# Second-norm rows ahead of the gated output, and the gate kept in PSUM, in a two-layer transformer kernel

## The chip, the cores and the metric

One core of a Trainium2 chip runs the whole program. The metric is the device time of one execution in microseconds. A core has TensorE (PE, with its weight loads PEld), VectorE (DVE), ScalarE (ACT), GpSimd (POOL) and SyncE (SP, which here issues DMAs), two on-chip memories (SBUF and PSUM, the second with 8 banks) and DMA queues. The engines run on their own and wait for each other by semaphores.

## What is computed

Two layers, each an attention and a mixture of experts, each behind an adaptive layer norm, on x of 8 x 512 rows by 256 columns (4096 rows, 32 tiles of 128). The change touches the first attention and the norm behind it:

```python
h = _layernorm(x, axis=-1) * (1 + ca) + sa
x = x + ga * _L0_attn_ref(h, W_Q, W_K, W_V, W_O)      # gated output, summed into x
h = _layernorm(x, axis=-1) * (1 + cb) + sb            # second norm: the "rows"

def _L0_attn_ref(query, W_Q, W_K, W_V, W_O):
    ...
    cos_KV = jnp.cumsum(cos_k * V, axis=1)
    sin_KV = jnp.cumsum(sin_k * V, axis=1)
    heads = cos_q * cos_KV + sin_q * sin_KV
    ...
    heads = heads / denom
    return jnp.einsum('deh,bthe->btd', W_O, heads)
```

`ga`, `sb` and `cb` are one row per batch entry, that is, per four tiles.

## The kernel before

Fp32 products are made of fp16 pairs: each operand is split into a high part and the low remainder (ScalarE rounds the high part, GpSimd subtracts it to get the low one), and three products are summed. X stays in SBUF for the whole program.

The first attention goes over 32 tiles in one loop, `for i in range(NT)`, written out by hand once for each engine. Nothing plans the order: it is the order of the lines in each engine's function, and semaphores tie them. In iteration i:

- TensorE (`tensor`) sums the scaled values of tile i along the sequence with a triangular matrix, in banks 0 to 3 (`tri`, 8 matmuls of 512 columns); turns the heads of tile i-1 (`turn_heads`, 8 transposes); multiplies the values of tile i+2 (`values`, 12 matmuls); except at a batch's end (i % 4 == 3), adds the rest of the tile into the banks for the next tile (`atri`, 8 matmuls), once VectorE has read the sums; projects the heads of tile i-1 (`heads_out`, 24 matmuls of 256 columns); at a batch's end it also spreads the second norm's scale and shift over the partitions (`by_batch`).
- VectorE (`vector`) reads the four banks and multiplies them by the queries' cosine and sine into TM (four instructions), makes the low part of tile i-1's turned heads (`heads_lo`, two), scales the first half of tile i+2's values (`spread`, two; these eight have 512 columns each), and adds the two halves of TM (1024 columns, both in SBUF; the head addition). Then `attended(i - 1)`: the gate (the projection in PSUM times GB, into the SBUF ring YG0), the add into X, and the moments of the new row (`moments`, two instructions); every fourth tile `factor`, a reciprocal of four columns. Last `rows(i - 5)` (R_AFTER is 5): two instructions that make the normed and modulated rows of a tile in the ring HR0.
- ScalarE (`scalar`) rounds the rows of tile i-6 (`rows_hi`) and the turned heads (`heads_hi`), scales the second half of the values of tile i+2 in 16 instructions, rounds the four pieces of the scaled values (`spread_hi`), takes a square root for a batch's four rows when their moments are there (`root`), and, from i = 3 to 26, rounds one piece of the experts' weights (`convert`, 1024 columns).
- GpSimd (`gpsimd`) makes the low parts of the same: `rows_lo` (256 columns), `spread_lo` (four of 512 columns) and `convert` (1024). Each reads two tensors in SBUF.
- SyncE loads and stores the pieces of the experts' weights, paced by GpSimd's `convert`, and stores the rows' pairs; after the loop, once the last projection is done, it loads the experts' weights.

The values, the projection and the spread scale and shift share two PSUM banks, 4 and 5, in a fixed order `VR`; `vr_free` (line 781) says what TensorE waits for before it writes a bank again. For a bank that held a projection that is the gate: `yg` counts two per tile, the gate and the add.

In the profile, VectorE's tensor-tensor instructions have line L1301 (the helper `tt`), told apart by shape and tiles: `BIG<-ps,BIG 128x256` is the gate, `X<-X,BIG` the add, `BIG<-BIG 128x1024` the head addition. L1447 and L1450 are the two instructions of `rows`, L1308 and L1310 the moments, L1315 the reciprocal. GpSimd's have L2297, ScalarE's scaling L1926 and its other copies L1852. TensorE's products have L736, its transposes in this loop L853. BIG is the large SBUF array of which most buffers are views, and ps is PSUM.

Of the kernel before, what the change touches and what calls it, by code (L numbers as in the profile page):

```python
# [8 lines left out]
ALU = mybir.AluOpType  # L9
# [3 lines left out]
B, S, D = 8, 512, 256  # L13
# [41 lines left out]
def bc(ap, axis, n):  # L55
    a = ap.unsqueeze(axis)
    shape = list(a.shape)
    shape[axis] = n
    return a.broadcast_to(shape)
# [9 lines left out]
def program(nc, x_in, wqk_in, wv_in, wo_in, rw_in, rb_in, w1_in, w3_in, w2_in, c0_in, m0_in,  # L69
# [3 lines left out]
    with ctx:  # L73
        def sb(name, shape, dt=fp32):
            return ctx.enter_context(nc.sbuf_tensor(name, shape, dt))
# [4 lines left out]
        s = {n: ctx.enter_context(nc.semaphore(n)) for n in SIGNALS}  # L80
# [12 lines left out]
        X = sb("X", [128, NT, D])  # L93
# [23 lines left out]
        ps = [ctx.enter_context(nc.psum_tensor(f"ps{i}", [128, 512], fp32)) for i in range(8)]  # L117

        def view(off, *shape, dt=None, parts=128):
            n = math.prod(shape)  # L120
            words = n // 2 if dt == f16 else n
            assert off + words <= BIGW, (off, shape)
            v = BIG[0:parts, off:off + words]
            return shaped(v.bitcast(dt) if dt is not None else v, shape)
# [35 lines left out]
        area = Area(22912)  # L160
# [4 lines left out]
        area = Area(0)  # L165
# [4 lines left out]
        cv_st, cv_pr = area.ring(2, 1024), area.pairs(2, 1024)  # L170

        cks = view(cv_at + 2048, 2, 2, NT, 16, dt=f16)
        YG0 = area.ring(2, D)
        GB = area(8, D)
        lap = area.at
        assert lap <= 22912, lap
        area = Area(lap)
# [18 lines left out]
        def kv_made(i, hf, j):  # L196

            if not by_act(i):
                return "kvf", 4 * i + 2 * hf + j + 1
            return ("kva", "kvf")[hf == 0], (8 if hf == 0 else 0) + 2 * (i - 2) + j + 1  # L200


        R_AFTER, R_SPLIT = 5, 6
# [24 lines left out]
        def heads_of(ap):  # L228
            return ap.rearrange("p (h e) -> p h e", e=64)
# [8 lines left out]
        vr_no = {u: i for i, u in enumerate(VR)}  # L238
# [117 lines left out]
        for l in range(2):  # L356
# [3 lines left out]
                y=[0, 0] if l == 0 else [16 * len(range(k, M[0].NS, 2)) for k in range(2)],  # L360
# [7 lines left out]
        area = Area(0)  # L368
# [18 lines left out]
        area = Area(33792)  # L387
        OI, OIT = area.ring(2, D), area.ring(2, 2, 2, 128, dt=f16)
        assert area.at <= 35584
        area = Area(35584)  # L390
        HF.append(area.pair(2, 2048))

        area = Area(36992)
# [338 lines left out]
        def tensor(e):  # L732
            pe = Lane(e)
# [47 lines left out]
            def vr_free(u):  # L781
                n = vr_no[u]
                if n < 2:
                    pe.wait_ge(s["modc"], 3)
                    return
                kind, i, hf = VR[n - 2]
                if kind == "v":
                    made, k = kv_made(i, hf, 1)
                    pe.wait_ge(s[made], k)
                elif kind == "s":  # L790
                    pe.wait_ge(s["sc"], i + 1)
                else:
                    pe.wait_ge(s["yg"], 2 * i + 1)

            def values(i):
                for hf in range(2):
# [11 lines left out]
            for t in range(A_TICKS):  # L808
                if t == T_PART:
                    mod_columns(1)  # L810
                if t in T_GB:
                    p = T_GB.index(t)
# [54 lines left out]
            for i in range(NT):  # L867
# [30 lines left out]
                if i % 4 == 3:  # L898
                    u = ("s", i // 4, 0)
                    vr_free(u)  # L900
                    pe.wait_ge(s["modg"], 8)
                    by_batch(ps[4 + vr_no[u] % 2], 0, 2, 4, i // 4).then_inc(s["sc_ps"], 1)
# [394 lines left out]
        def vector(e):  # L1297
            dve = Lane(e)

            def tt(o, a, b, op):  # L1300
                return e.tensor_tensor(o, a, b, op)  # L1301

            def moments(n, i):

                r = n % 4
                if n >= 4:
                    dve.wait_ge(s["bn"], 2 * (n - 4) + 2)
                e.bn_stats(bnst[:, r, :], X[:, i, :]).then_inc(s["bn"], 1)  # L1308
                dve.wait_ge(s["bn"], 2 * n + 1)
                e.bn_aggr(stat[:, i, :], bnst[:, r, :]).then_inc(s["bn"], 1)  # L1310

            def factor(g, dev):

                dve.wait_ge(s["rs_a"], g + 1)
                e.reciprocal(dev, dev).then_inc(s["rs_v"], 1)  # L1315
# [6 lines left out]
            def row(i):  # L1322
                return rstd[:, i - 3:i + 1]
# [31 lines left out]
            def divide(h):  # L1355

                cut = slice(16 * h, 16 * h + 16)
                cumc, cums = (cumb[h][:, j].rearrange("p b c n -> p (b c) n") for j in range(2))
                dn, d2 = (TH[:, cut, :].rearrange(FLAT)[:, 256 * k:256 * k + 256].rearrange("p (t n) -> p t n", n=16) for k in range(2))
                dve.wait_ge(s["kc_ps"], h + 1)  # L1360

                dve.wait_ge(s["th"], 3 * h + 3)
                c = Serial(dve, s["dn"], 6 * h)
                tt(dn, QC[:, cut, 0:16], cumc, ALU.mult).then_inc(c.next(), 1)
                n = c.next()
                tt(d2, QS[:, cut, 0:16], cums, ALU.mult).then_inc(n, 1)
                n = c.next()
                e.scalar_tensor_tensor(out=dn, in0=dn, scalar=1e-6, in1=d2, op0=ALU.add, op1=ALU.add).then_inc(n, 1)
                n = c.next()
                e.reciprocal(dn, dn).then_inc(n, 1)  # L1370
                n = c.next()
                tt(QC[:, cut, 0:16], QC[:, cut, 0:16], dn, ALU.mult).then_inc(n, 1)
                n = c.next()
                tt(QS[:, cut, 0:16], QS[:, cut, 0:16], dn, ALU.mult).then_inc(n, 1)
# [42 lines left out]
            def heads_lo(i):  # L1417
                for q in range(2):
                    dve.wait_ge(s["ht_hi"], 2 * i + q + 1)
                    tt(HT[i % 2][1][:, 4 * q:4 * q + 4, :], ps[6 + q][:, :].rearrange("p (j n) -> p j n", j=4),  # L1420
                       HT[i % 2][0][:, 4 * q:4 * q + 4, :], ALU.subtract).then_inc(s["ht_lo"], 1)

            def attended(i):
                dve.wait_ge(s["pr_ps"], i + 1)
                dve.wait_ge(s["gr"], 4)
                if i >= 2:
                    dve.wait_ge(s["yg"], 2 * (i - 2) + 2)
                tt(YG0[i % 2], ps[4 + vr_no["p", i, 0] % 2][:, 0:256], GB[:, i // 4, :], ALU.mult).then_inc(s["yg"], 1)
                dve.wait_ge(s["yg"], 2 * i + 1)
                tt(X[:, i, :], X[:, i, :], YG0[i % 2], ALU.add).then_inc(s["yg"], 1)  # L1430
                dve.wait_ge(s["yg"], 2 * i + 2)
                moments(NT + i, i)
                if i and i % 4 == 0:
                    factor(8 + i // 4 - 1, row(i - 1))

            def rows(n):

                b = n // 4
                dve.wait_ge(s["rs_v"], 8 + b + 1)
                dve.wait_ge(s["sc"], b + 1)  # L1440
                if n >= 4:
                    dve.wait_ge(s["hs_lo"], n - 3)
                else:

                    dve.wait_ge(s["dn"], 12)
                h, sc = HR0[n % 4], SC[b % 2]
                e.scalar_tensor_tensor(out=h, in0=X[:, n, :], scalar=stat[:, n, 0:1], in1=sc[:, 256:512],  # L1447
                                       op0=ALU.subtract, op1=ALU.mult).then_inc(s["hr"], 1)
                dve.wait_ge(s["hr"], 2 * n + 1)
                e.scalar_tensor_tensor(out=h, in0=h, scalar=rstd[:, n:n + 1], in1=sc[:, 0:256],  # L1450
                                       op0=ALU.mult, op1=ALU.add).then_inc(s["hr"], 1)

            for i in range(NT):
                dve.wait_ge(s["cum"], i + 1)
                dve.wait_ge(s["dn"], 6 if i < 16 else 12)
                if i >= 2:
                    dve.wait_ge(s["hdT_ps"], 2 * (i - 2) + 2)
                tm = TM[i % 2]
                for j, q in ((0, QC), (1, QS)):
                    for hf in range(2):  # L1460
                        tt(heads_of(tm[:, j, hf * 512:hf * 512 + 512]), heads_of(ps[2 * j + hf][:, :]),
                           bc(q[:, i, 8 * hf:8 * hf + 8], 2, 64), ALU.mult).then_inc(s["rd"], 1)
                if i:
                    heads_lo(i - 1)
                if i + 2 < NT:
                    spread(i + 2)
                dve.wait_ge(s["rd"], 4 * i + 4)
                tt(tm[:, 0], tm[:, 0], tm[:, 1], ALU.add).then_inc(s["hd"], 1)
                if i == 0:
                    divide(1)  # L1470
                if i:
                    attended(i - 1)
                if i >= R_AFTER:
                    rows(i - R_AFTER)
            heads_lo(NT - 1)


# [1112 lines left out]

        block = ctx.enter_context(nc.Block())
        block.vector(vector)
        block.sync(sync)
        block.gpsimd(gpsimd)
# [32 lines left out]
```

## Time and profile before

| what | value |
|---|---|
| median of 3 runs | 1909.5 us (1907.44 to 1913.1) |
| the profiled execution, its own time | 1908.69 us |
| its span | 1906.9 us |
| TensorE busy in the span | 1605.1 us (84%) |
| VectorE busy | 1180.3 us (62%) |
| GpSimd busy | 1088.0 us (57%) |
| ScalarE busy | 968.2 us (51%) |
| DMA | 204.16 MB, mean 107 GB/s |

The span runs from the first to the last instruction of the profiled execution; the rest of its time lies around it. Busy times overlap, so their shares say only how full an engine is over the whole program, whose stages differ. The attention loop that the change touches runs from about 76 to 462 us of the span; routing, the first experts (from 548 us), the second attention, and the second experts follow.

### The profile page before, as it was taken

To read this page: it belongs to the slowest core of one execution; us is meant where nothing else is said; L and a number is where in the kernel's file an instruction comes from. 1 tells how busy PE (TensorE), PEld (TensorE's weight loads), DVE (VectorE), ACT (ScalarE), POOL (GpSimd) and SP (SyncE) were. 2 spreads that over 40 slices of the span, in tenths; PEclk is the share of its full clock that TensorE was granted. 3 is DMA by queue.
4 is the path that set the end of the run, shared out by engine and by line. 5 is a ranking of instruction groups with operands and counts; after the bars stand their busy time and mean duration, and the time that the engine had idled before them with its cause. 6 is when DMAs were issued, how large, how long until landed. Compare 5 with 4: busy or idle time off the path is not lost.

```text
span 1906.9 us, 38349 instructions
## 1 busy us (share of the span) xinstructions
PE 1605.1 (84%) x13740; PEld 1179.2 (62%) x13740; DVE 1180.3 (62%) x1766; ACT 968.2 (51%) x2400; POOL 1088.0 (57%) x949
## 2 busy tenths in 40 slices
PE   6798878877799999999999927878887867599992
PEld 5454444445688888888888813334443325599992
DVE  7777787777543333333444376899999998422224
ACT  6675665564344444444454347544443436355553
POOL 5566556653133333333453289899997995355543
PEclk9899898899599999999999966989998997699996
DMA  5013332311733333333343150011110244366665
GB/s 200 23 45 97 100 93 83 100 59 61 263 95 101 101 99 100 98 99 98 115 157 95 51 176 23 1 28 29 29 29 25 73 146 125 132 237 245 232 236 185
DMA packets 130625, 204.16 MB, mean 107 GB/s; under 512 B 44864, under 2 KB 90960, under 8 KB 125328
## 3 DMA queue, kind: packets, MB, share of 16 engines
q1 hardware_dynamic: 114368, 132.22, 22.1%
q0 software_dynamic: 16080, 69.48, 10.8%
q8 instruction: 123, 2.02, 0.4%
q14 instruction: 54, 0.44, 0.1%
HBM read 138.09 MB, written 63.57 MB: 106 GB/s over the span
## 4 chain that ended last, share of the span: by engine, by line
PE 57%; DVE 17%; POOL 12%; issue 7%; ACT 2%; DMA 2%; SPq 0%; POOLq 0%; DVEq 0%; ACTq 0%
PE ps L736 55%; POOL BIG L2297 10%; DVE BIG L1301 9%; DVE X L1301 2%; DVE BIG L1801 2%; DMA BIG<-YT 1%; ACT BIG L1852 1%; DVE bnst L1308 1%; DVE BIG L1447 1%; POOL BIG L2501 1%; PE ps L1017 1%; POOL X L2297 1%; DVE BIG L1779 1%; PE ps L1086 0%; DMA BIG<-HB,BIG 0%
## 5 line engine op out<-in xcount | busy, mean ns | idle before, releaser
L736 PE MATMUL ps<-BIG 128*128 128x256 f16 (+9 forms) x11272 | 1294.7, 289 | 142.0 <-DVE BIG L1301 52.1
L736 PEld LDWEIGHTS ps<-BIG 128*128 128x128 f16 (+3 forms) x11272 | 973.1, 101 | 427.8 <-issue 77.1
L2297 POOL TENSOR_TENSOR BIG<-BIG 128x256 f16<-128x256 f32 (+6 forms) x547 | 751.6, 1406 | 488.1 <-ACT BIG L1852 466.9
L1852 ACT ACTIVATE BIG<-BIG 128x512 f16<-128x512 f32 (+3 forms) x543 | 329.9, 658 | 300.4 <-DVE BIG L1301 181.5
L1301 DVE TENSOR_TENSOR BIG<-BIG 128x512 f16<-128x512 f32 (+9 forms) x334 | 265.9, 804 | 273.7 <-ACT BIG L1852 266.3
L1852 ACT ACTIVATE BIG<-ps 128x64 f32<-128x64 f32 (+7 forms) x791 | 275.5, 409 | 266.1 <-PE ps L736 236.2
L1301 DVE TENSOR_TENSOR BIG<-ps,BIG 128x512 f32<-128x512 f32 (+3 forms) x421 | 290.4, 745 | 82.0 <-PE ps L736 80.6
L1301 DVE TENSOR_TENSOR BIG<-BIG,ps 128x512 f32<-128x512 f32 (+2 forms) x212 | 125.0, 594 | 262.7 <-PE ps L736 246.6
L2439 POOL DMA_INDIRECT YT<-BIG x109 | 108.7, 998 | 191.1 <-ACT BIG L1852 190.4
L1801 DVE TENSOR_REDUCE BIG<-BIG 128x160 f32<-128x2560 f32 x64 | 182.0, 2843 | 0.0
L2433 POOL DMA_INDIRECT BIG<-HB,BIG x109 | 108.3, 994 | 70.0 <-DVE BIG L1301 38.6
L2210 ACT ACTIVATE ps<-ps 128x512 f32<-128x512 f32 x64 | 37.2, 582 | 138.9 <-PE ps L736 138.9
L1926 ACT ACTIVATE BIG<-ps,BIG 128x64 f32<-128x64 f32 x480 | 101.4, 368 | 12.4 <-PE ps L736 12.0
L2068 ACT ACTIVATE BIG<-ps 128x512 f32<-128x512 f32 x140 | 81.9, 585 | 12.1 <-PE ps L736 12.1
L736 PE MATMUL ps<-BIG,atri 128*128 128x512 f16 x192 | 52.8, 425 | 29.3 <-DVE BIG L1301 29.3
L2117 ACT ACTIVATE BIG<-ps 128x512 f32<-128x512 f32 x78 | 46.6, 597 | 41.8 <-PE ps L736 38.7
L1779 DVE TENSOR_REDUCE BIG<-ps 128x32 f32<-128x512 f32 x64 | 43.7, 682 | 33.3 <-PE ps L736 32.4
L736 PE MATMUL ps<-BIG,tri 128*128 128x512 f16 (+1 forms) x264 | 63.1, 377 | 0.9 <-DVE BIG L1301 0.9
L2217 ACT ACTIVATE BIG<-ps 128x512 f32<-128x512 f32 x64 | 38.4, 600 | 36.6 <-DVE BIG L1801 36.5
L736 PEld LDWEIGHTS ps<-BIG,atri 128*128 128x128 f16 x192 | 18.9, 107 | 61.3 <-DVE BIG L1301 38.4
L1308 DVE BATCH_NORM_STATS2 bnst<-X 128x6 f32<-128x256 f32 x128 | 54.2, 423 | 3.9 <-DMA X<-in_x 2.1
L2468 POOL DMA_INDIRECT BIG<-WG,BIG x39 | 37.3, 955 | 27.0 <-DVE BIG L1301 13.5
(139 smaller groups left out, 955.6 us busy)
## 6 DMA issues: line engine op xcount, KB each, us to landing
WD<-BIG SPq DMA_DIRECT2D x80, 256.0 KB, 2.4
BIG<-in_v SPq DMA_DIRECT2D x32, 512.0 KB, 4.6
BIG<-in_w SPq DMA_DIRECT2D x24, 512.0 KB, 4.0
BIG<-WD SPq DMA_DIRECT2D x32, 384.0 KB, 7.6
BIG<-YT SPq DMA_DIRECT2D x24, 512.0 KB, 5.0
HB<-BIG SPq DMA_DIRECT2D x64, 128.0 KB, 2.5
WG<-BIG SPq DMA_DIRECT2D x32, 256.0 KB, 3.2
BIG<-WD SPq DMA_DIRECT2D x16, 512.0 KB, 5.3
```

The lines of the kernel that those rows point to most:

```text
L736: return e.matmul(o, lhsT, rhs, start=start, stop=stop, skip_group_check=True)
L1301: return e.tensor_tensor(o, a, b, op)
L1308: e.bn_stats(bnst[:, r, :], X[:, i, :]).then_inc(s["bn"], 1)
L1779: e.tensor_reduce(SM[q % 4], shaped(ps[2 + q % 3][:, :], (2, 16, 16)), AX.X, ALU.max).then_inc(s["sm"], 1)
L1801: e.tensor_reduce(OB[c % 2][:, 2 * q2:2 * q2 + 2], PV[q % 2], AX.X, ALU.add).then_inc(s["vr"], 1)
L1852: return e.activation(o, i, ACT.Copy)
L1926: o = e.activation(KVF[i % 2][:, j, 512 + 64 * h:576 + 64 * h], ps[4 + vr_no["v", i, 1] % 2][:, 64 * h:64 * h + 64], ACT.Copy, scale=q[:, ...
L2068: e.activation(m_.UP[u % 2], ps[2 * u % 4][:, :], ACT.Silu).then_inc(s["su"], 1)
L2117: e.activation(m_.UP[j % 2][:, hf * 512:hf * 512 + 512], ps[idx % 4][:, :], ACT.Gelu).then_inc(s["su"], 1)
L2297: return e.tensor_tensor(o, a, b, op)
L2433: e.indirect_dma_start(m_.HIN[t % ring], None, m_.HB, bass.IndirectOffsetOnAxis(m_.gi[:, t:t + 1], 0)).then_inc(ld_hi[t % ring], 16)
L2439: e.indirect_dma_start(m_.YT, bass.IndirectOffsetOnAxis(m_.yi[:, t:t + 1], 0), m_.YO[t % 2], None).then_inc(st_y[t % 2], 16)
```

## The change

In VectorE's loop the order behind the head addition becomes: the reciprocal of the batch before (in iterations 5, 9, 13 and so on, as before, but ahead of the rest), the rows of tile i-5, and then the gate, the add and the moments of tile i-1. The gate writes its result over the projection in PSUM instead of into the SBUF ring YG0, and the add into X reads it there. YG0 (512 words per partition) goes, and so does the wait for it; the buffers placed behind it move down. TensorE waits for the add instead of the gate before it writes that bank again.

```diff
@@ -170,7 +170,6 @@
         cks = view(cv_at + 2048, 2, 2, NT, 16, dt=f16)
-        YG0 = area.ring(2, D)
         GB = area(8, D)
@@ -790,7 +789,7 @@
                 else:
-                    pe.wait_ge(s["yg"], 2 * i + 1)
+                    pe.wait_ge(s["yg"], 2 * i + 2)
@@ -1423,15 +1422,12 @@
             def attended(i):
                 dve.wait_ge(s["pr_ps"], i + 1)
                 dve.wait_ge(s["gr"], 4)
-                if i >= 2:
-                    dve.wait_ge(s["yg"], 2 * (i - 2) + 2)
-                tt(YG0[i % 2], ps[4 + vr_no["p", i, 0] % 2][:, 0:256], GB[:, i // 4, :], ALU.mult).then_inc(s["yg"], 1)
+                y = ps[4 + vr_no["p", i, 0] % 2][:, 0:256]
+                tt(y, y, GB[:, i // 4, :], ALU.mult).then_inc(s["yg"], 1)
                 dve.wait_ge(s["yg"], 2 * i + 1)
-                tt(X[:, i, :], X[:, i, :], YG0[i % 2], ALU.add).then_inc(s["yg"], 1)
+                tt(X[:, i, :], X[:, i, :], y, ALU.add).then_inc(s["yg"], 1)
                 dve.wait_ge(s["yg"], 2 * i + 2)
                 moments(NT + i, i)
-                if i and i % 4 == 0:
-                    factor(8 + i // 4 - 1, row(i - 1))
@@ -1468,10 +1464,12 @@
                 if i == 0:
                     divide(1)
+                if i % 4 == 1 and i > 1:
+                    factor(8 + i // 4 - 1, row(i - 2))
+                if i >= R_AFTER:
+                    rows(i - R_AFTER)
                 if i:
                     attended(i - 1)
-                if i >= R_AFTER:
-                    rows(i - R_AFTER)
             heads_lo(NT - 1)
```

## Rows read from the trace of the kernel before

**Rows 1.** The page: the span.
```profile
span 1906.9 us, 38349 instructions
```

**Rows 2.** Busy time by stretch; columns: stretch, its length, each engine's busy us, clock, DMA.
```profile
98.50:127.50 29.00, 27.49 (x182) 17.48 (x181) 22.95 (x40) 21.61 (x69) 16.15 (x14) 1.00 0.12 38
...
179.60:231.20 51.60, 41.73 (x240) 24.65 (x240) 40.83 (x62) 31.80 (x100) 31.61 (x25) 0.90 0.31 92
...
548.00:1066.00 518.00, 518.00 (x4865) 461.73 (x4863) 207.17 (x264) 237.78 (x392) 201.12 (x168) 1.00 0.34 106
```

**Rows 3.** VectorE's groups, 89 to 480 us: busy us, mean ns of one, idle before.
```profile
L1450 DVE SCALAR_TENSOR_TENSOR BIG<-BIG,rstd 128x256 f32<-128x256 f32 x32 | 37.2, 1161 | 1.1
L1301 DVE TENSOR_TENSOR X<-X,BIG 128x256 f32<-128x256 f32 x32 | 33.9, 1059 | 1.1
...
L1301 DVE TENSOR_TENSOR BIG<-ps,BIG 128x256 f32<-128x256 f32 x32 | 13.6, 425 | 74.7 <-PE ps L736 74.7
```

**Rows 4.** VectorE in order of time, iterations 11 to 15: start us, duration us, instruction.
```profile
203.47 4.86 DVE L1301 TENSOR_TENSOR BIG<-ps,BIG 128x512 f32<-128x512 f32 x8
...
216.78 0.45 DVE L1447 SCALAR_TENSOR_TENSOR BIG<-X,stat,BIG 128x256 f32<-128x256 f32 x1
217.27 0.48 DVE L1450 SCALAR_TENSOR_TENSOR BIG<-BIG,rstd 128x256 f32<-128x256 f32 x1
217.67 4.87 DVE L1301 TENSOR_TENSOR BIG<-ps,BIG 128x512 f32<-128x512 f32 x8
222.46 1.22 DVE L1301 TENSOR_TENSOR BIG<-BIG 128x1024 f32<-128x1024 f32 x1
225.43 0.42 DVE L1301 TENSOR_TENSOR BIG<-ps,BIG 128x256 f32<-128x256 f32 x1 [1.75 <-PE ps L736]
...
228.93 4.87 DVE L1301 TENSOR_TENSOR BIG<-ps,BIG 128x512 f32<-128x512 f32 x8
...
239.81 2.23 DVE L1450 SCALAR_TENSOR_TENSOR BIG<-BIG,rstd 128x256 f32<-128x256 f32 x1
...
254.98 1.28 DVE L1301 TENSOR_TENSOR BIG<-ps,BIG 128x512 f32<-128x512 f32 x2
```

**Rows 5.** GpSimd in order of time, in iterations 12 and 13.
```profile
223.14 5.08 POOL L2297 TENSOR_TENSOR BIG<-BIG 128x512 f16<-128x512 f32 x4 [4.18 <-ACT BIG L1852]
...
238.15 3.60 POOL L2297 TENSOR_TENSOR BIG<-BIG 128x512 f16<-128x512 f32 x2
```

**Rows 6.** All engines in order of time, iterations 3 and 4, which make no rows.
```profile
108.07 4.88 DVE L1301 TENSOR_TENSOR BIG<-ps,BIG 128x512 f32<-128x512 f32 x8
...
113.00 2.79 PE L736 MATMUL ps<-BIG 128*128 128x256 f16 x24 [1.51 <-DVE BIG L1301]
...
118.00 4.88 DVE L1301 TENSOR_TENSOR BIG<-ps,BIG 128x512 f32<-128x512 f32 x8 [0.38 <-PE ps L736]
...
120.16 2.13 POOL L2297 TENSOR_TENSOR BIG<-BIG 128x1024 f16<-128x1024 f32 x1
...
121.47 3.38 ACT L1926 ACTIVATE BIG<-ps,BIG 128x64 f32<-128x64 f32 x16 [1.94 <-PE ps L736]
...
125.44 2.46 POOL L2297 TENSOR_TENSOR BIG<-BIG 128x512 f16<-128x512 f32 x2 [3.16 <-ACT BIG L1852]
125.61 1.89 PE L736 MATMUL ps<-BIG,tri 128*128 128x512 f16 x8
125.81 0.42 DVE L1301 TENSOR_TENSOR BIG<-ps,BIG 128x256 f32<-128x256 f32 x1 [1.80 <-PE ps L736]
...
127.54 0.69 DVE L1301 TENSOR_TENSOR BIG<-ps,BIG 128x512 f32<-128x512 f32 x1
```

**Rows 7.** The page's groups: ScalarE from PSUM to PSUM, and to SBUF.
```profile
L2210 ACT ACTIVATE ps<-ps 128x512 f32<-128x512 f32 x64 | 37.2, 582 | 138.9 <-PE ps L736 138.9
...
L2217 ACT ACTIVATE BIG<-ps 128x512 f32<-128x512 f32 x64 | 38.4, 600 | 36.6 <-DVE BIG L1801 36.5
```

**Rows 8.** VectorE in order of time: the start of iteration 30.
```profile
443.39 3.67 DVE L1301 TENSOR_TENSOR BIG<-ps,BIG 128x512 f32<-128x512 f32 x6
```

## The prediction

> **What bounds the kernel now.** I read five things in turn: the span, the busy table of the attention loop, the groups of VectorE's instructions there, one stretch of the loop in order of time, and the five iterations that have no second-norm rows yet. The profiled execution took 1908.69 us, 1.79 us of it outside its span [rows 1]; the median of the three runs shown is 1909.5, so I sum against 1908.7 and add 0.8.
>
> In a stretch of 51.6 us of the loop no engine is full: TensorE is busy 41.7 us, VectorE 40.8, ScalarE 31.8, GpSimd 31.6, and TensorE's granted clock is 0.90 [rows 2]. So a chain across engines sets the pace. Four iterations (i = 11 to 14) run from 203.47 to 254.98: 51.5 us, 12.9 each [rows 4].
>
> The chain stands in one iteration in order of time [rows 4]. It starts at S, when VectorE begins to read the cumulative sums. Eight instructions follow, then the addition of the two heads' halves, finished at S+6.0 (217.67 to 223.68). VectorE then idles 1.75 us until TensorE's projection of the tile before is there (225.43, S+7.8), gates it, adds it into X, takes moments, makes the rows, and only then starts the next iteration (228.93). The rows stand behind the late arrival although their inputs are five tiles old.
>
> Two kinds of instruction on that chain last much longer than their work. The add into X takes 1059 ns in the mean, the gate of the same shape, which reads one operand from PSUM, 425; the rows' second instruction takes 1161 in the mean [rows 3] and 0.48 at its shortest [rows 4]. Where it took 2.23 (239.81 to 242.04), GpSimd was running two subtractions from 238.15 to 241.75 [rows 5]: VectorE ended 0.3 us behind it. An instruction whose two tensors both lie in SBUF waits for GpSimd's current one; the gate never does, since 425 is the mean of all 32.
>
> Iterations 3 and 4, which make no second-norm rows, show what the loop can do without this [rows 6]. Iteration 4 lasted 9.54 us (118.00 to 127.54) and iteration 3 9.93 (108.07 to 118.00); the second has no `atri` product and ends a batch, and TensorE waited 1.51 us in it. TensorE's cumulative sum for iteration 5 ran 125.61 to 127.50, straight behind its projection, and VectorE started at 127.54: both engines are full there, at clock 1.00 [rows 2]. That is the floor: 9.54 for three iterations of four, 9.93 for the fourth.
>
> **The change, part by part.** Rows are made in iterations 5 to 31.
>
> (a) The rows move into the idle time. Uncontended they cost 0.45 + 0.48 = 0.93 us [rows 4], once in four with a reciprocal of four columns more (some 0.1 us, an estimate), against 1.75 us idle: S+6.0 to S+7.0 or 7.1. Behind the projection there remain gate, add, moments. In iteration 4 this chain lasted 125.81 to 127.54, 1.73 us, with an add of 0.60.
>
> (b) The add reads PSUM and X: one SBUF tensor, so the shape of the gate, 0.425 [rows 3]. That takes 0.63 off its mean, and 0.18 off the chain just named: 1.73 - 0.18 = 1.55. VectorE could start again at S+7.8+1.55 = S+9.35, before TensorE's sum at 9.5. So TensorE sets the pace.
>
> (c) The gate writes PSUM. No VectorE row of this loop does. The nearest pair is ScalarE's, PSUM to PSUM 582 ns against PSUM to SBUF 600 [rows 7]. I take 0.42; bounds 0.40 and, doubled, 0.85. The double would make the chain 1.98 and the iteration 9.8. Adding the same doubt for the add's PSUM read gives 10.2.
> The Trainium skill (VectorE: DVE Perf Modes, the section on the TRN2 errata) gives a PSUM source 62 cycles more than an SBUF one, some 0.065 us, which speaks against moving the operand. The trace doesn't show it for this shape: the gate takes 0.425 [rows 3], and the add in iterations 1 to 4 was no shorter. By the page the chain is 1.62 instead of 1.55, 27 times 0.065 or 1.8 us if all of it were exposed, and nothing of it under the 9.54 floor.
>
> (d) Does GpSimd leave that gap free? It depends on when its hi/lo subtractions start. Now they start at 223.14, S+5.5 [rows 5], because VectorE is late against TensorE; in iteration 4 they started at 125.44, S+7.4, since ScalarE's scaling began only at 121.47, S+3.5 [rows 6]. The rows end at S+7.1 and fit. GpSimd's long subtraction of the weight conversion came at 120.16 to 122.29, S+2.2 to S+4.3, before the head addition at S+4.8; the rows' own subtraction behind it, about 0.7 (an estimate from the 1.27 of one twice as wide) reaches S+5.0 to 5.3, delays the head addition by up to 0.5 and the rows' end to 7.6: still under 7.8. Should VectorE fall behind by 1.5 us, as now, the rows get held once or twice: S+8.8, restart at S+10.35. TensorE then also runs late by about as much, GpSimd starts later relative to VectorE, and the next iteration is back near 9.5. So the state without collisions holds itself up.
>
> (e) Waits. TensorE's next user of the gate's PSUM buffer now waits for the add, 0.45 us later than the gate. The add is done at S+8.7; that user is the values' second half (or, at a batch's end, the first), which comes behind the cumulative sum and the turned heads, so not before S' = S+9.5. Covered by 0.8 us at least; without cover, 0.45 per iteration, 12 us in all. ScalarE's square root waits for moments that end at S+9.3, and before at S+10 or later, behind the long add. ScalarE's copy of the rows waits for rows that are made earlier by the whole idle time and the add. Queued behind both are the conversions and the turned heads, so these gain too. The dropped wait for the ring of gated tiles never held (same engine, in order): 0. SyncE and the DMA queues issue the same transfers, paced by GpSimd's subtractions; 9.5 us per piece is what iterations 3 and 4 already had. 512 words of SBUF freed: 0.
>
> (f) The sum. Iterations 5 to 29 run from 127.54 to 443.39 [rows 6, 8]: 315.85 us. After: 19 x 9.54 + 6 x 9.93 = 240.8. Gain 75.0. Iterations 30 and 31 lose the 0.93 us behind the gate: 1.9. Together 77, of which 20 us is the add (32 x 0.63), 25 the rows without collisions (27 x 0.93), 18 the collisions of their second instruction (27 x 0.68), and the rest the clock at 0.90 and the first instruction's. Behind the loop everything waits for its end (weights are fetched only after the last projection), and the experts' 518 us run at clock 1.00 with TensorE busy 518.0 [rows 2], so the stages after only move. 1908.7 - 77 + 0.8 = 1832.5; I say 1833.
>
> **The rivals.**
> A, the forecast: the loop goes at TensorE's floor, 1833; with (c)'s bounds and a little jitter 1827 to 1842.
>
> B, the collisions move along. The rows now stand right behind the head addition, where GpSimd starts its four subtractions, 5.08 us together [rows 5]. If it keeps starting at S+5.5, the first holds the rows to S+7.0, the second to 8.4, they end at 8.8, and the chain to 10.35. 19 x 0.8 = 15 us more: 1848. Against it: (d). Against that: (d) is an argument on the order of events that no row shows with rows in the loop.
> The Trainium skill (SBUF — State Buffer, Who interferes with whom) states this lock: the pair of ports is held for a whole instruction, and a VectorE instruction with one SBUF input stays out of it. The trace agrees with both halves [rows 3, 5]; applied without (d) it gives B's 1848.
>
> C, part of the gain isn't there: another chain, ScalarE's (3.38 us scaling, then its copies) or the fetching of weights to convert, holds the iteration at 11.3, which is the shortest that an iteration with rows has now (217.67 to 228.93). 25 x 11.3 = 282: gain 33, with the tail 35: 1874. For it: ScalarE is busy 31.8/4 = 8 us of a 9.5 us iteration. Against: it did the scaling and the copies in iterations 3 and 4 too, at 9.5 to 9.9.
>
> D, slower. The rows stand ahead of the gate, so whatever holds them holds TensorE, through the add. Held for 2.2 us each, they end at S+10.4, chain 1.55: 12.0, still under today's 12.6 (315.85/25). It decides only if gate and add, whose PSUM bank neighbours the ones that TensorE writes, take over 0.6 us more together. At 1.3 us each they add 1.75: 13.75 x 25 = 344, 28 us more: 1937. No row has such a PSUM access.
>
> E, no change: the loop's gain is taken back in the routing or expert stages, or the rows wait for the same late work as the gate, so that moving them changes nothing. Against: they read X of five tiles back, and the later stages wait for the loop's last products: 1909.
>
> **Chances.** A 0.65, B 0.20, C 0.10, D 0.02, E 0.03. The range, 1825 to 1854, takes in A and B with (c)'s bounds on the high side, and leaves out C, D, E. Faster by over 0.3% (what a measurement of this kernel can tell from no change, 5.7 us): 0.95; within: 0.03; slower: 0.02.
>
> **What the profile would show.** Starts of iterations 9.5 us apart, 9.9 at each fourth; TensorE's clock 1.00 from 127 us on; the add at 0.42 in all 32, the gate between 0.40 and 0.5; the rows at 0.45 and 0.48 directly behind the head addition, still idle time of some 0.7 us before the gate; GpSimd's four subtractions starting at S+7.4 instead of S+5.5; VectorE ready just before TensorE's sum. I am wrong if the rows show 0.7 to 2.2 us again before the gate (B), if TensorE waits while VectorE waits too (C), if gate or add are over 0.6 (c, D), or if a later stage is longer.

## The result and the profile after

The changed kernel takes 1833.47 us in the median of 4 runs (1828.91 to 1835.46), the kernel before 1908.97 beside it. The ratio is 0.9598, with a 95% interval from 0.9574 to 0.9621: 4% faster. The forecast was 1833, with a range from 1825 to 1854. The profiled execution has a span of 1831.8 us, 75.1 less than [rows 1].

Busy time in iterations 11 to 14, now 38.6 us instead of 51.5; the columns are those of [rows 2]:

```profile
187.49:226.04 38.55, 37.04 (x242) 23.44 (x241) 34.20 (x62) 31.49 (x99) 28.90 (x25) 1.00 0.40 124
```

TensorE is busy 37.0 of 38.6 us at clock 1.00; before it was busy 41.7 of 51.6 at 0.90 [rows 2]. ScalarE's busy time is about that of before (31.5 us, 31.8 before). VectorE's fell from 40.8 to 34.2 and GpSimd's from 31.6 to 28.9: an instruction that is held counts as busy, and there are fewer of these now.

VectorE's groups in the loop, to be read against [rows 3]:

```profile
L1300 DVE TENSOR_TENSOR BIG<-BIG 128x1024 f32<-128x1024 f32 x31 | 41.1, 1326 | 0.0
...
L1446 DVE SCALAR_TENSOR_TENSOR BIG<-BIG,rstd 128x256 f32<-128x256 f32 x32 | 16.4, 512 | 1.1
...
L1300 DVE TENSOR_TENSOR ps<-ps,BIG 128x256 f32<-128x256 f32 x32 | 13.8, 433 | 29.7 <-PE ps L735 29.7
...
L1300 DVE TENSOR_TENSOR X<-X,ps 128x256 f32<-128x256 f32 x32 | 13.5, 421 | 1.1
```

The rows' second instruction (now L1446) fell from 1161 ns to 512, and the add from 1059 to 421. The gate that writes PSUM takes 433 where the gate that wrote SBUF took 425. VectorE's idle time before it fell from 74.7 us to 29.7: the rows fill some 26 us of it (27 times 0.96), and the projection no longer comes late at a batch's end, as shown below. The head addition became longer, 1326 ns against 1212: it now sometimes waits for GpSimd.

Iteration 12 in order of time, the counterpart of [rows 4] and [rows 5]:

```profile
197.43 4.88 DVE L1300 TENSOR_TENSOR BIG<-ps,BIG 128x512 f32<-128x512 f32 x8 [0.61 <-PE ps L735]
...
200.89 3.38 ACT L1924 ACTIVATE BIG<-ps,BIG 128x64 f32<-128x64 f32 x16 [1.78 <-PE ps L735]
202.22 1.22 DVE L1300 TENSOR_TENSOR BIG<-BIG 128x1024 f32<-128x1024 f32 x1
202.42 2.78 PE L735 MATMUL ps<-BIG 128*128 128x256 f16 x24
203.35 0.48 DVE L1443 SCALAR_TENSOR_TENSOR BIG<-X,stat,BIG 128x256 f32<-128x256 f32 x1
203.87 0.48 DVE L1446 SCALAR_TENSOR_TENSOR BIG<-BIG,rstd 128x256 f32<-128x256 f32 x1
...
204.87 3.40 POOL L2295 TENSOR_TENSOR BIG<-BIG 128x512 f16<-128x512 f32 x3 [2.72 <-ACT BIG L1850]
205.04 1.89 PE L735 MATMUL ps<-BIG,tri 128*128 128x512 f16 x8
205.24 0.43 DVE L1300 TENSOR_TENSOR ps<-ps,BIG 128x256 f32<-128x256 f32 x1 [0.89 <-PE ps L735]
205.71 0.42 DVE L1300 TENSOR_TENSOR X<-X,ps 128x256 f32<-128x256 f32 x1
206.16 0.43 DVE L1307 BATCH_NORM_STATS2 bnst<-X 128x6 f32<-128x256 f32 x1
206.62 0.18 DVE L1309 BATCH_NORM_AGGREGATE stat<-bnst 128x2 f32<-128x6 f32 x1
...
206.97 0.69 DVE L1300 TENSOR_TENSOR BIG<-ps,BIG 128x512 f32<-128x512 f32 x1 [0.16 <-PE ps L735]
```

The rows run from 203.35 to 204.35, S+5.9 to S+6.9, behind the head addition; then VectorE still idles 0.89 us. GpSimd starts its four at 204.87, S+7.4, when the rows are done. The moments end at 206.80, and the next iteration starts at 206.97, released by TensorE's sum: 9.54 us after 197.43. Before, this iteration took 11.26.

The starts of iterations 5 and 30:

```profile
129.85 1.29 DVE L1300 TENSOR_TENSOR BIG<-ps,BIG 128x512 f32<-128x512 f32 x2 [0.16 <-PE ps L735]
...
370.70 1.89 DVE L1300 TENSOR_TENSOR BIG<-ps,BIG 128x512 f32<-128x512 f32 x3 [0.16 <-PE ps L735]
```

240.85 us lie between them, 315.85 before [rows 6, 8]: 75.0 less. Iteration 30 lost 1.97 us more (10.80 to 8.83). This execution had reached iteration 5 2.3 us later than the one before, already behind in the loading of x; the stages after the loop differ by 0.4 us. So the whole gain is in the loop.

A part of it is TensorE's clock. This is the projection at the batch's end of iteration 11, before and after:

```profile
208.39 5.10 PE L736 MATMUL ps<-BIG 128*128 128x256 f16 x24 [4.18 <-DVE BIG L1301]
```

```profile
192.42 2.79 PE L735 MATMUL ps<-BIG 128*128 128x256 f16 x24 [1.51 <-DVE BIG L1300]
```

Before, TensorE had stood idle for 4.18 us, and from 207.9 to 213.6 its granted clock was 0.54, near the lower of its two levels (1.2 GHz, the other is 2.4). The same 24 matmuls took 5.10 us instead of 2.79, and VectorE waited for them. The six projections at the batches' ends between iterations 5 and 30 took 4.35 to 5.25 us each, 13.0 us more in all than at 2.79. In the changed kernel the idle time there is 1.51 us, and the clock stays at 1.00 from iteration 5 to 30. So some 13 of the 75 us came through the clock. No run here sets it apart from the holds that delay TensorE.

### The profile page after: what moved, and what is told of

It is laid out like the page before. It is cut to its first block, busy times and chain, and to the rows that moved or that the text cites. A ratio compares the mean times of both kernels' runs of the same rounds, so it can differ in the third digit from the quotient of the medians.

```text
span 1831.8 us, 38349 instructions
## 1 busy us (share of the span) xinstructions
PE 1578.2 (86%) x13740; PEld 1173.7 (64%) x13740; DVE 1139.9 (62%) x1766; ACT 967.2 (53%) x2400; POOL 1071.8 (59%) x949
## 4 chain that ended last, share of the span: by engine, by line
PE 64%; POOL 13%; DVE 9%; issue 5%; DMA 2%; ACT 2%; SPq 0%; POOLq 0%; DVEq 0%; ACTq 0%
PE ps L735 61%; POOL BIG L2295 11%; DVE BIG L1300 5%; DVE BIG L1799 2%; DMA BIG<-YT 1%; PE ps L852 1%; POOL BIG L2499 1%; PE ps L1016 1%; ACT BIG L1850 1%; POOL X L2295 1%; DMA BIG<-HB,BIG 1%; PE ps L1085 0%; DVE BIG L1777 0%; DMA HB<-BIG 0%; PE ps L912 0%
## 5 line engine op out<-in xcount | busy, mean ns | idle before, releaser
L735 PE MATMUL ps<-BIG 128*128 128x256 f16 (+9 forms) x11272 | 1280.9, 287 | 116.5 <-DVE BIG L1777 45.1
L2295 POOL TENSOR_TENSOR BIG<-BIG 128x256 f16<-128x256 f32 (+6 forms) x547 | 736.0, 1382 | 426.9 <-ACT BIG L1850 409.4
L1300 DVE TENSOR_TENSOR BIG<-BIG 128x512 f16<-128x512 f32 (+9 forms) x334 | 269.8, 816 | 278.2 <-ACT BIG L1850 274.5
L1300 DVE TENSOR_TENSOR BIG<-ps,BIG 128x512 f32<-128x512 f32 (+2 forms) x389 | 277.0, 774 | 15.1 <-PE ps L735 13.8
L2066 ACT ACTIVATE BIG<-ps 128x512 f32<-128x512 f32 x140 | 81.9, 585 | 12.3 <-PE ps L735 12.1
L1155 PE MATMUL ps<-ident,BIG 128*128 128x128 f32 x64 | 17.7, 381 | 36.9 <-DVE BIG L1325 19.5
L735 PE MATMUL ps<-BIG,atri 128*128 128x512 f16 x192 | 45.4, 379 | 3.1 <-DVE BIG L1300 3.1
```

What stands on the lines that cost most here:

```text
L735: return e.matmul(o, lhsT, rhs, start=start, stop=stop, skip_group_check=True)
L2066: e.activation(m_.UP[u % 2], ps[2 * u % 4][:, :], ACT.Silu).then_inc(s["su"], 1)
```

## The experiments

Eight other kernels ran, and the changed kernel and one of the eight a second time; each ratio is to runs of the kernel before on the same chip.

### The two parts, each alone

`e1_order` is the kernel before with the new order only; gate and add keep the SBUF ring:

```diff
-                if i and i % 4 == 0:
-                    factor(8 + i // 4 - 1, row(i - 1))
...
+                if i % 4 == 1 and i > 1:
+                    factor(8 + i // 4 - 1, row(i - 2))
+                if i >= R_AFTER:
+                    rows(i - R_AFTER)
                 if i:
                     attended(i - 1)
-                if i >= R_AFTER:
-                    rows(i - R_AFTER)
```

> The order alone: rows ahead of the gate, the gated tile still in the SBUF ring. Theory: the loop goes at TensorE's floor of 9.54 us an iteration, and the order is what brings it there. The add is held by GpSimd's subtraction that starts at S+7.44 and takes 0.60 instead of 0.42, the chain behind the projection 1.73 instead of 1.55, which just fits: S+7.8+1.73=S+9.54. So 1834 to 1838, nearly the whole gain. Rival, the two parts add up (20 us of the gain for the add's 0.63 us in 32 iterations): 1853.

Measured: 1833.72 us (1831.74 to 1838.51) against 1909.67, ratio 0.9605 (0.9565 to 0.9645). This is the time of the full change. Its iteration 12 behind the projection:

```profile
204.56 0.42 DVE L1301 TENSOR_TENSOR BIG<-ps,BIG 128x256 f32<-128x256 f32 x1 [0.89 <-PE ps L736]
205.02 0.61 DVE L1301 TENSOR_TENSOR X<-X,BIG 128x256 f32<-128x256 f32 x1
...
206.29 1.29 DVE L1301 TENSOR_TENSOR BIG<-ps,BIG 128x512 f32<-128x512 f32 x2
```

The add takes 0.61: GpSimd's subtraction, begun before it, ends at 205.35, and the add 0.28 us behind that. VectorE goes on to the next iteration at 206.29 without an idle moment; TensorE's sum was just ready. Iterations 5 to 29 all last 9.54 or 9.94 us. What PSUM buys is the 0.16 us of idle time that the changed kernel shows at 206.97, which nothing uses.

`e2_psum` is the kernel before with the gate in place and the add from PSUM (and TensorE's later wait), rows still last:

```diff
...
-                if i >= 2:
-                    dve.wait_ge(s["yg"], 2 * (i - 2) + 2)
-                tt(YG0[i % 2], ps[...][:, 0:256], GB[:, i // 4, :], ALU.mult).then_inc(s["yg"], 1)
+                y = ps[4 + vr_no["p", i, 0] % 2][:, 0:256]
+                tt(y, y, GB[:, i // 4, :], ALU.mult).then_inc(s["yg"], 1)
                 dve.wait_ge(s["yg"], 2 * i + 1)
-                tt(X[:, i, :], X[:, i, :], YG0[i % 2], ALU.add).then_inc(s["yg"], 1)
+                tt(X[:, i, :], X[:, i, :], y, ALU.add).then_inc(s["yg"], 1)
```

> The PSUM operand alone: gate in place, add from PSUM, rows still behind the moments. Theory: the add is short (0.42) but the rows, both in SBUF, now meet the same GpSimd subtractions a little earlier and are held in its place; the iteration stays at 11 to 13 us, and 5 to 20 us are gained: 1889 to 1904, with the rows' first instruction longer in the mean than the 0.605 us of before. Rival, the parts add up: the full 20 us, 1889, and the rows as long as before.

Measured: 1908.06 us (1905.25 to 1909.85), ratio 0.9987 (0.9972 to 1.0002): at most 0.3%, under both expectations. The mechanism of the theory holds, its size doesn't. VectorE's groups from 89 to 430 us:

```profile
L1449 DVE SCALAR_TENSOR_TENSOR BIG<-BIG,rstd 128x256 f32<-128x256 f32 x23 | 36.7, 1594 | 0.8
L1446 DVE SCALAR_TENSOR_TENSOR BIG<-X,stat,BIG 128x256 f32<-128x256 f32 x23 | 28.5, 1241 | 0.2
...
L1301 DVE TENSOR_TENSOR X<-X,ps 128x256 f32<-128x256 f32 x27 | 11.3, 420 | 0.9
```

The kernel before, in the same stretch:

```profile
L1301 DVE TENSOR_TENSOR X<-X,BIG 128x256 f32<-128x256 f32 x28 | 31.3, 1118 | 1.0
L1450 DVE SCALAR_TENSOR_TENSOR BIG<-BIG,rstd 128x256 f32<-128x256 f32 x23 | 31.1, 1354 | 0.8
...
L1447 DVE SCALAR_TENSOR_TENSOR BIG<-X,stat,BIG 128x256 f32<-128x256 f32 x23 | 14.8, 645 | 0.2
```

One iteration of `e2_psum` in order of time, VectorE alone:

```profile
224.03 0.42 DVE L1301 TENSOR_TENSOR X<-X,ps 128x256 f32<-128x256 f32 x1
...
225.04 1.43 DVE L1446 SCALAR_TENSOR_TENSOR BIG<-X,stat,BIG 128x256 f32<-128x256 f32 x1
226.50 2.38 DVE L1449 SCALAR_TENSOR_TENSOR BIG<-BIG,rstd 128x256 f32<-128x256 f32 x1
```

The add is down to 0.42, and the next two instructions, both with two SBUF tensors, wait instead. The adds (28 and 27 of them in the stretch) gave up 31.3 - 11.3 = 20.0 us; the rows took (28.5 - 14.8) + (36.7 - 31.1) = 19.3. The same wait was passed on to the next instructions of its kind, whole: from iteration 5 to 30 the loop took 315.3 us instead of 315.85.

### Is it a hold for the whole of GpSimd's instruction?

`e3_quarters` is the kernel before with GpSimd's 1024-column subtraction of the loop cut into four; the order on VectorE is untouched:

```diff
...
-                tt(pr[c % 2][1][:, 0:w], st[c % 2][:, 0:w], pr[c % 2][0][:, 0:w], ALU.subtract).then_inc(s["cv_lo"], 1)
...
+                    for k in range(4):
+                        cut = slice(256 * k, 256 * k + 256)
+                        m = tt(pr[c % 2][1][:, cut], st[c % 2][:, cut], pr[c % 2][0][:, cut], ALU.subtract)
+                    m.then_inc(s["cv_lo"], 1)
```

> The kernel before, with GpSimd's long subtraction of the weight pieces (1024 columns, 2.13 us) cut into four of 256. Theory: a VectorE instruction with two SBUF tensors waits for GpSimd's current instruction to end, whole. Then the longest of the adds and rows falls from 2.2 us to about 1, three iterations of four are 1.2 us shorter, 24 batches' iterations in all: about 1886. Rival, the engines share a rate and only total work counts: the long instructions stay at 2 us and the time at 1909 or above.

Measured: 1884.41 us (1880.45 to 1888.99), ratio 0.9871 (0.9828 to 0.9913), where the theory said 1886. VectorE and GpSimd in the loop:

```profile
L2297 POOL TENSOR_TENSOR BIG<-BIG 128x256 f16<-128x256 f32 x128 | 89.4, 725 | 29.8 <-ACT BIG L1852 29.8
...
L1301 DVE TENSOR_TENSOR X<-X,BIG 128x256 f32<-128x256 f32 x32 | 30.2, 944 | 1.1
L1450 DVE SCALAR_TENSOR_TENSOR BIG<-BIG,rstd 128x256 f32<-128x256 f32 x32 | 25.7, 803 | 1.1
```

The rows' second instruction, 2.23 us behind the long subtraction [rows 4], is 0.78 at the same place, and 803 ns in the mean. GpSimd does the same work in more instructions, and VectorE is held less: the hold lasts to the end of GpSimd's current instruction. This cut alone was worth 25 us of the 76. From iteration 5 to 30 the loop took 293.1 us, 22.8 less. Take what VectorE's instructions with two SBUF tensors (adds, rows and head additions) last beyond their shortest duration: that sum is 45.2 us in the kernel before and 30.7 here, 14.5 less. And the projections at the batches' ends lose 8.1 us to the lower clock instead of 13.0, since TensorE stands idle for less time ahead of them.

### How much slack the new order has, and what lies past it

`e4_one_more` and `e5_two_more` are the changed kernel with one or two instructions more (0.48 us each, two SBUF tensors, results unused) between rows and gate; `e8_one_behind` has one behind the moments (and ScalarE waits for it before it writes that scale anew). The edit of `e4_one_more`:

```diff
                     rows(i - R_AFTER)
+                    n = i - R_AFTER
+                    for k in range(1):    # e5_two_more: range(2), and 2 * (n - 1) below
+                        dve.wait_ge(s["xd"], max(1 * (n - 1) + k + 1, 0))
+                        e.scalar_tensor_tensor(out=XD[k], in0=X[:, n, :], scalar=stat[:, n, 0:1], in1=SC[n // 4 % 2][:, 256:512],
+                                               op0=ALU.subtract, op1=ALU.mult).then_inc(s["xd"], 1)
                 if i:
                     attended(i - 1)
```

> The changed kernel with one more instruction like the rows' first (0.48 us, two SBUF tensors, result unused) behind the rows and ahead of the gate, in iterations 5 to 31. Both theories: it fits in the 0.5 to 0.9 us that VectorE idles there: 1833 to 1836.

Measured: 1833.11 us (1831.4 to 1834.95), ratio 0.9613 (0.9594 to 0.9632). It is free. In iteration 12 it takes the idle time's place, 0.49 left of 0.89:

```profile
203.61 0.48 DVE L1475 SCALAR_TENSOR_TENSOR BIG<-X,stat,BIG 128x256 f32<-128x256 f32 x1
204.57 0.43 DVE L1301 TENSOR_TENSOR ps<-ps,BIG 128x256 f32<-128x256 f32 x1 [0.49 <-PE ps L736]
```

> The same with two more instructions, 0.96 us, 0.1 to 0.5 us more than the idle time. Theory: the second meets GpSimd's first subtraction (start S+7.44) and is held for up to 1.1 us; VectorE falls behind, GpSimd starts earlier against it, more instructions are held, and the loop falls back into the state of the kernel before: iterations of 10.5 to 12 us, 1860 to 1895. Rival, only the surplus over the idle time counts: 27 times 0.1 to 0.5 us, 1836 to 1847.

Measured: 1878.42 us (1872.62 to 1880.46), ratio 0.984 (0.9814 to 0.9866): 45 us more for 13 us of work (27 times 0.48), inside the theory's range and far outside the rival's. Iterations 13 and 14 of it, VectorE:

```profile
227.43 2.74 DVE L1475 SCALAR_TENSOR_TENSOR BIG<-X,stat,BIG 128x256 f32<-128x256 f32 x2
230.09 0.42 DVE L1301 TENSOR_TENSOR ps<-ps,BIG 128x256 f32<-128x256 f32 x1
...
237.47 1.39 DVE L1444 SCALAR_TENSOR_TENSOR BIG<-X,stat,BIG 128x256 f32<-128x256 f32 x1
238.88 1.26 DVE L1447 SCALAR_TENSOR_TENSOR BIG<-BIG,rstd 128x256 f32<-128x256 f32 x1
240.07 2.67 DVE L1475 SCALAR_TENSOR_TENSOR BIG<-X,stat,BIG 128x256 f32<-128x256 f32 x2
```

and its GpSimd:

```profile
227.43 7.58 POOL L2301 TENSOR_TENSOR BIG<-BIG 128x512 f16<-128x512 f32 x6 [2.12 <-ACT BIG L1856]
236.97 8.39 POOL L2301 TENSOR_TENSOR BIG<-BIG 128x512 f16<-128x512 f32 x6 [1.95 <-ACT BIG L1856]
```

GpSimd starts at 227.43, S+7.4, the pair behind it takes 2.74 us instead of 0.96, and the gate, which could have run at 227.8, when the projection was done, runs at 230.09. VectorE starts the next iteration 2 us behind TensorE's sum. There GpSimd starts at 236.97, S+5.4, as in the kernel before, and all four instructions are held: 12.57 us for the iteration. Of the 44.8 us that the loop lost between iterations 5 and 30, 11.7 are projections at the lower clock. It isn't a trap for good, but VectorE's lateness doesn't end it by itself: iterations 5 to 11 lasted 10.3, 10.9, 11.7, 11.7, 11.9, 12.6 and 12.6 us. Iterations 12, 20, 24 and 28 were back at 9.5. They are those behind a batch's end at which the projection took 5.30 us (granted clock 0.50), so that TensorE was late enough for VectorE to catch up. Behind the ends at which it took 2.79 (iteration 7) and 4.46 (iteration 15) the loop stayed at 11.7 and 11.9.

> The changed kernel with the same extra instruction (0.48 us, two SBUF tensors, result unused) behind the moments instead of ahead of the gate, where it cost nothing. Theory: it begins at S+9.3, inside GpSimd's subtractions (S+7.44 on), is held for up to 1.1 us, makes VectorE late, and the loop falls back to iterations of 10.4 to 11.5 us: 1855 to 1885. Rival, only its own length over a slack of 0.2 us counts: 27 times 0.28, 1841.

Measured: 1832.1 us (1830.55 to 1834.69), ratio 0.9596 (0.9578 to 0.9614): no slower than the changed kernel. Both expectations missed. Two iterations of it, VectorE:

```profile
206.78 0.71 DVE L1477 SCALAR_TENSOR_TENSOR BIG<-X,stat,BIG 128x256 f32<-128x256 f32 x1
...
216.65 0.45 DVE L1477 SCALAR_TENSOR_TENSOR BIG<-X,stat,BIG 128x256 f32<-128x256 f32 x1
```

It was held 0.26 us at 206.78, not a full subtraction; VectorE fell 0.43 behind, so GpSimd's boundaries came at S+7.06 instead of 7.45, and in the next iteration the instruction fell right between two of them (0.45, no hold) and VectorE caught up to 0.16. Between iterations 5 and 30 this cost 245.3 - 240.8 = 4.5 us. The median doesn't show it, and the rest of this execution behind iteration 30 was 3.0 us shorter than the changed kernel's on that chip, which I can't tell from scatter: over all the kernels here that rest lies between 1456 and 1464 us.

`after_again` is the changed kernel, run beside the last three kernels:

> The changed kernel once more, beside the next three on one chip: 1833, iterations of 9.54 and 9.94 us.

Measured: 1832.31 us (1825.86 to 1833.78), ratio 0.959 (0.9568 to 0.9611).

### A faster version

TensorE still waits 1.5 us at each batch's end. `e6_batch_end` moves VectorE's second pair of readings behind the two things that TensorE waits for there:

```diff
-                for j, q in ((0, QC), (1, QS)):
+                def read(j, q):
                     for hf in range(2):
...
+                read(0, QC)
+                if i % 4 != 3:
+                    read(1, QS)
                 if i:
                     heads_lo(i - 1)
                 if i + 2 < NT:
                     spread(i + 2)
+                if i % 4 == 3:
+                    read(1, QS)
```

> The changed kernel, and at each batch's end (i % 4 == 3) VectorE makes the low heads and scales the values ahead of the second half of its reading of the sums, since TensorE doesn't wait for that reading there but for the other two. Theory: TensorE's 1.51 us of idle time in these iterations falls to about 0.3, the iteration from 9.94 to 8.8: 7 to 8 times 1.1, some 8 us less than the changed kernel, 1825. Rival: VectorE or ScalarE is late next and holds the iteration after it at over 9.54: 1830 to 1834.

Measured: 1826.5 us (1824.21 to 1829.16), ratio 0.9559 (0.9522 to 0.9596). The batch's last iteration is 9.30, not the expected 8.8, so it gave 0.64 us per batch and not 1.1. TensorE in it:

```profile
189.59 2.79 PE L735 MATMUL ps<-BIG 128*128 128x256 f16 x24 [0.31 <-DVE BIG L1300]
...
192.77 0.62 PE L735 MATMUL ps<-ident,MC 128*128 128x128 f16 x8 [0.38 <-ACT BIG L1929]
```

The wait before the projection fell from 1.51 to 0.31 as said. A new one came behind it: 0.38 us for ScalarE, whose scaling of the values frees the bank of the spread scale. Once more beside the others:

> The batch-end order once more, beside the changed kernel: its loop was 3.9 us shorter between the starts of iterations 5 and 30 (6 times 0.65), so 1826 to 1829 where the changed kernel has 1833.

Measured: 1825.67 us (1823.66 to 1831.55), ratio 0.9565 (0.9544 to 0.9586): 6.6 us under the changed kernel on this chip. The traces show 3.8 of them between iterations 5 and 30 and 0.65 in iteration 3; the other 2 us I can't tell from scatter.

`e7_scale_later` adds to it that TensorE spreads the scale behind the next iteration's sum:

```diff
                 m.then_inc(s["cum"], 1)
+                if i % 4 == 0 and i:
+                    spread_scale(i // 4 - 1)
...
-                if i % 4 == 3:
-                    u = ("s", i // 4, 0)
-                    vr_free(u)
-                    pe.wait_ge(s["modg"], 8)
-                    by_batch(ps[4 + vr_no[u] % 2], 0, 2, 4, i // 4).then_inc(s["sc_ps"], 1)
```

> The batch-end order, and TensorE spreads the next norm's scale behind the next iteration's cumulative sum instead of ahead of it, since at the batch's end it waited 0.38 us there for ScalarE to free the bank. Theory: that wait goes and the batch-end iteration falls from 9.29 to 8.9: 7 times 0.38, 1824. Rival: the heads' turn and ScalarE's work start 0.5 us later, VectorE waits for the turned heads in the iteration after, and nothing is gained: 1826 to 1829.

Measured: 1820.76 us (1818.2 to 1824.6), ratio 0.9531 (0.9513 to 0.955), 11.55 us under the changed kernel's 1832.31 on the same chip and lower than either expectation. TensorE and VectorE around a batch's end:

```profile
188.81 2.79 PE L735 MATMUL ps<-BIG 128*128 128x256 f16 x24 [0.31 <-DVE BIG L1304]
...
191.44 1.89 PE L735 MATMUL ps<-BIG,tri 128*128 128x512 f16 x8
...
193.17 0.61 PE L735 MATMUL ps<-ident,MC 128*128 128x128 f16 x8
...
196.26 2.48 DVE L1304 TENSOR_TENSOR BIG<-ps,BIG 128x512 f16<-128x512 f32 x4 [0.19 <-ACT BIG L1859]
```

The sum follows the projection at once, and the scale's wait is gone. The rival was right in part: VectorE now waits 0.19 us for the turned heads in the next iteration. The two iterations took 8.53 + 9.75 = 18.28 us where `e6_batch_end` had 9.30 + 9.54 = 18.84: 0.56 less per batch. From iteration 5 to 30: 240.8 in the changed kernel, 237.0 in `e6_batch_end`, 233.7 here. With 1.2 us in iterations 3 and 4 the traces show 8.3 us of the 11.55; the rest I can't tell from scatter.

## Why the prediction was right

**The floor.** That the loop would go at TensorE's 9.54 and 9.93 us of iterations 3 and 4 was the step that carried the number: 240.8 said, 240.85 measured, the granted clock 1.00 throughout. That 25 more iterations would behave like two was an inference from [rows 6]; the profile shows it for each. That the median came within 0.5 us of the forecast is luck: the four runs lie 6.5 us apart, and the predicted gain was 77 us where 75.5 was measured. The 1.5 us are no more than the 2.3 us by which the profiled execution was late before the loop.

**(a), the rows in the idle time.** Right: 0.48 + 0.48 us at S+5.9 to S+6.9, and 0.5 to 0.9 us of idle time left. `e1_order` shows that the order alone is the whole gain.

**(b), the add.** Its duration was right (0.425 said, 0.421 measured), and so was the chain behind the projection, 1.55 said, 1.56 measured (205.24 to 206.80). But the text gave the add 20 of the 77 us, by 32 times 0.63. That is wrong: alone it brings nothing (`e2_psum`, ratio 0.9987), and beside the order nothing (`e1_order`). The failed step is the split of the sum in (f), not the sum, which was made from iteration lengths. Likewise the 25 and 18 us for rows and collisions are no separate gains; that some 25 us hang on the longest holds is what `e3_quarters` measured. The rest of the sum, 14 us, was put to the clock and the rows' first instruction without a working; the slow projections at the batches' ends are 13.0 us of that kind. What the order took away shows in the traces as one thing: what VectorE's instructions with two SBUF tensors last beyond their shortest duration, from iteration 5 to 30, is 45.2 us in the kernel before, 45.5 in `e2_psum`, 12.1 in `e1_order` and 4.2 in the changed kernel. `e1_order` is as fast as the changed kernel in spite of its 12.1, because these holds don't reach past TensorE's sum.

**(c), the gate into PSUM.** 433 ns against 425: the value taken. VectorE's add with a PSUM operand took 421 ns where the shortest one out of SBUF took 424. The 62 cycles that the Trainium skill (VectorE: DVE Perf Modes, the section on the TRN2 errata) gives a PSUM source more don't show in these durations.

**(d), GpSimd out of the way.** Right: in every iteration from 5 to 29 the four subtractions start at S+7.44, where before they started at S+5.4 to 5.7 from iteration 6 to 27. The delay of the head addition was put at up to 0.5 us; in the mean it is 0.11 (1326 ns against 1212). That being on time keeps GpSimd out of the way, and being late brings it in, was argued; `e5_two_more` shows the second half. The way back was too simple: (d) has TensorE run late by about as much, so that the next iteration is near 9.5 again. In `e5_two_more` seven iterations in a row grew instead, from 10.3 to 12.6 us, and the way back was open only behind a projection of 5.30 us. With 0.43 us of lateness (`e8_one_behind`) the next iteration did catch up. For the changed kernel itself (d)'s recovery isn't shown, since it never fell behind in its two traces. B was this state, and it lay closer than its 0.20 says in one respect: one instruction more fits, two don't.

**(e), the waits.** TensorE has no wait for the add; its only ones left are the 1.51 us at each batch's end.

**(f), the ends.** 1.9 us for iterations 30 and 31 together; iteration 30 alone gave 1.97, and iteration 31 with all that follows it 0.4. The later stages only moved.

**C, D, E.** ScalarE didn't limit the loop at 9.54, but it is what comes next: it limits `e6_batch_end` at the batch's end. No access to PSUM was slow.

## What to carry to other kernels

When two engines contend for SBUF by whole instructions, count an instruction's hold with the chain that it lies on, and then look at who inherits it: a shorter operand path for one instruction passes the wait to the next one of its kind. Move work whose inputs are old ahead of a late arrival, into the idle time, and check that it ends before the other engine starts its burst; when that brings the pacing engine back to no idle time at all, the iterations that already run so give the new time better than a sum of durations does. Then measure the slack with a dummy instruction: here 0.48 us more were free and 0.96 cost 45 us.

## What the runs showed of the hardware

An extra instruction behind the moments, inside GpSimd's burst, was held 0.26 us and then not at all (`e8_one_behind`): VectorE's lateness shifts GpSimd's boundaries against it, and with one such instruction the two settle between them, with two in a row before the gate they don't. And cutting one subtraction of 2.2 us in the mean into four of 0.74, 3.0 us together and so more time on GpSimd, made the whole kernel 25 us faster with VectorE's order untouched (`e3_quarters`). Idle time of TensorE cost a second time through its clock: behind 4.18 us of idle time its granted clock was 0.54, and a projection took 5.10 us; behind 1.51 us it was 1.00, and the same took 2.79 (iteration 11, before and after).
